# One Trainium2 core, decoder block: a merged opening, cross-attention scores by key, value products in three fp16 parts

## The reference

```python
x = x + attn(layernorm(x))                    # 128 heads, content 4 wide, rotary part 64 wide
x = x + xattn(layernorm(x), ctx, ctx, pos)    # 32 heads of 16, 8 key/value heads, rotary positions
x = x + ffn(layernorm(x))                     # 512x512 product, bias, top 2 of 8 low-rank experts
# cross-attention:
q = rope((x @ Wq)); k = rope((ctx @ Wk)); v = ctx @ Wv     # k, v repeated for 4 query heads each
probs = softmax(q @ k.T / 4)
x_out = (probs @ v) @ Wo
```

## Time and profile before

| | us |
|---|---|
| three runs | 902.01, 900.76, 896.24; median 900.76 |
| profiled execution, device time | 899.96 |
| its span, first to last instruction | 898.2 |
| busy in the span | PE 831.3, DVE 661.5, ACT 615.3, POOL 584.6 |
| mean granted TensorE clock | 0.974 of full |

### The profile page before, as it was taken

The page is one execution under the profiler, slowest core; times in us unless marked ns, Lnnn a source line. Parts: engine busy times, 40 slices in busy tenths (PEclk is TensorE's granted clock), DMA queues, the critical chain, the costliest instruction groups (busy, mean ns, idle before and its releaser), DMA issues. The chain is left out here.

```text
span 898.2 us, 18249 instructions
## 1 busy us (share of the span) xinstructions
PE 831.3 (93%) x5720; PEld 425.4 (47%) x5720; DVE 661.5 (74%) x1225; ACT 615.3 (68%) x1253; POOL 584.6 (65%) x491
## 2 busy tenths in 40 slices
PE   4968999999999999999999999999848889999996
PEld 3444444444444444444444444444313556666552
DVE  7877676767777888777888776887556667888764
ACT  4744777777777777777777777776602777777761
POOL 7824888878888887888788888876523341333210
PEclk9988999999999999999999999999979988999999
DMA  8341545543443334334333434422120000000000
GB/s 322 112 153 21 169 122 142 156 121 86 99 121 95 92 80 109 87 105 121 87 82 87 113 97 105 118 57 64 26 71 1 1 1 2 13 13 13 14 13 36
DMA packets 50719, 74.66 MB, mean 83 GB/s; under 512 B 9457, under 2 KB 33009, under 8 KB 50161
## 3 DMA queue, kind: packets, MB, share of 16 engines
q1 hardware_dynamic: 50672, 74.11, 29.7%
HBM read 38.16 MB, written 18.87 MB: 63 GB/s over the span
## 5 line engine op out<-in xcount | busy, mean ns | idle before, releaser
L480 POOL TENSOR_TENSOR Pl<-PR,Ph 128x512 f16<-128x512 f32 x254 | 286.2, 1158 | 30.0 <-ACT Ph L657 30.0
L650 ACT ACTIVATE PR<-PS 128x512 f32<-128x512 f32 x256 | 152.5, 597 | 129.7 <-PE PS L1266 123.2
L898 DVE TENSOR_REDUCE mneg<-PS 128x4 f32<-128x512 f32 x256 | 174.6, 685 | 38.2 <-PE PS L1246 34.7
L1197 PE MATMUL PS<-XTh,Wh 128*128 128x512 f16 x512 | 195.4, 382 | 0.0
L1197 PE MATMUL PS<-XTh,Wl 128*128 128x512 f16 x512 | 194.5, 380 | 0.0
L1197 PE MATMUL PS<-XTl,Wh 128*128 128x512 f16 x512 | 194.2, 379 | 0.0
L775 DVE SCALAR_TENSOR_TENSOR QS<-PS,QC 64x512 f16<-64x512 f32 x256 | 175.5, 686 | 18.9 <-ACT QC L578 11.9
L578 ACT ACTIVATE QC<-PS 64x512 f16<-64x512 f32 x256 | 150.7, 589 | 10.6 <-PE PS L1197 4.3
L657 ACT ACTIVATE Ph<-PR 128x512 f16<-128x512 f32 x256 | 139.3, 617 | 0.0
L1246 PEld LDWEIGHTS PS<-KC,QC 112*128 112x128 f16 x1024 | 79.0, 98 | 65.0 <-issue 5.9
L462 POOL TENSOR_TENSOR Wh<-Wraw,wscale 128x1024 f16<-128x1024 f32 x32 | 60.6, 1894 | 70.8 <-PE PS L1197 67.5
(11 more groups left out here) (211 smaller groups left out, 1281.8 us busy)
## 6 DMA issues: line engine op xcount, KB each, us to landing
Wraw<-in_wqr SPq DMA_DIRECT2D x32, 512.0 KB, 4.6
QS<-QC SPq DMA_DIRECT2D x64, 256.0 KB, 3.1
head_outputs<-OS SPq DMA_DIRECT2D x256, 40.0 KB
q_content_parts<-stg SPq DMA_DIRECT2D x12, 256.0 KB, 2.9
k_content_parts<-stg SPq DMA_DIRECT2D x12, 256.0 KB, 3.0
QC<-q_content_parts SPq DMA_DIRECT2D x128, 24.0 KB
KC<-k_content_parts SPq DMA_DIRECT2D x32, 96.0 KB
xs<-in_x SPq DMA_DIRECT2D x8, 256.0 KB, 4.7
```

The costliest lines, as they stand in the source:

```text
L480: nc.gpsimd.tensor_tensor(Pl[:, b], PR[:, b % 4], Ph[:, b], ALU.subtract).then_inc(s_pl, 1)
L650: nc.scalar.activation(PR[:, b % 4, :], PS[:, bB[b % 2], :], ACT.Exp, scale=ATT_SCALE).then_inc(s_e, 1)
L898: nc.vector.tensor_reduce(mneg[:, par, b // 4, :, b % 4], PS[:, bA[b % 2], :].rearrange("p (j k) -> p j k", j=GH), AX.X, ALU.max, negate=T ...
L1197: last = mm(PS[:, bQ[c % 2], :], wt[:, par, k, p * P:(p + 1) * P], xt[:, k, sl], start=(k == 0 and n == 0), stop=(k == KT - 1 and n == 2))
```

## The change

1. Opening: step 0 is gone. Each of the last four rounds of the loop over b on PE also issues one `rough_scores(0, 0, b - 4)`, with `row_max` behind the round's `up_low` on DVE; the first `max_turn` moves into step 1 behind its first projection, behind waits for the last `up_low` and `v_low`. The angles move to DVE's step 32, Sin to ACT behind the first weight split after the loop, the tables and both `k_rope` to DVE behind the weight splits. SP no longer waits for the key copies, and issues the first `q_again` by itself.
2. Second part: a unit's rough scores (8 products, both halves' row groups by turns), two maxima, one transpose of [128, 8] maxima, an ACT copy `xmT`, two small DMAs into row 48 of each half of `KQ`, scores by key (4 products of 256 columns, maximum subtracted by that row), Exp in 2 instructions of 512, high parts on ACT, low parts on POOL, and 12 fp16 value products. The 8 fp32 transposes of probabilities, their copies, the 8 Exp of 128 and the fp32 value product go. Rough scores run two units ahead. `x_back` comes behind `turn`. `KQ` has four buffers.
3. POOL writes high and low parts of `xvz`, and 16 into column 48 of `kst`. SP's result stores stand between the maxima's DMAs.

```diff
@@ -399,13 +401,12 @@
             contents(1, 1)
             store(1)
             store(2)
-            sp.wait_ge(s_kc, 2)
-            spelled(step, 0, 1)
+            q_again(0, 0, 0)
+            spelled(step, 1, 1)
             store(3)
             spelled(step, 2, 2)
...
-            for b in range(B):
+            def x_maxima(u):
+                sp.wait_ge(s_xme, u + 1)
+                for h in range(2):
+                    row = XROW * h + X3
+                    sp.dma_start(KQ[row:row + 1, u % 4, 0:UQ, :], xmT[REP * h:REP * (h + 1), u % 2, :]).then_inc(s_xmd[u % 2], 16)
+
...
+            for u in range(NU):
+                x_maxima(u)
+                if u % KT == KT - 1 and u // KT >= 3:
+                    result(u // KT - 3)
+            for b in range(B - 3, B):
+                result(b)
...
-            nc.gpsimd.memset(kst[:], 0.0)
+            nc.gpsimd.memset(kst[:], 0.0).then_inc(s_kx, 1)
             nc.gpsimd.memset(xvz[:], 0.0).then_inc(s_xvz, 1)
             nc.gpsimd.memset(qst[:], 0.0).then_inc(s_kx, 1)
+            pool.wait_ge(s_kx, 2)
+            nc.gpsimd.memset(kst[:, :, :, :, X3], MS).then_inc(s_kx, 1)
             pool.wait_ge(s_xvz, 1)
-            nc.gpsimd.tensor_copy(xvz[:, :, :, 0:XVC], xv[:]).then_inc(s_xvz, 1)
-            pool.wait_ge(s_kx, 1)
+            nc.gpsimd.tensor_copy(xvz[:, 0, :, :, 0:XVC], xv[:]).then_inc(s_xvz, 1)
+            pool.wait_ge(s_xvz, 2)
+            nc.gpsimd.tensor_tensor(xvz[:, 1, :, :, 0:XVC], xv[:], xvz[:, 0, :, :, 0:XVC], ALU.subtract).then_inc(s_xvz, 1)
+            pool.wait_ge(s_kx, 3)
...
@@ -564,6 +583,10 @@
                     nc.gpsimd.tensor_tensor(part[1], k, part[0], ALU.subtract).then_inc(s_kst, 1)
                 if r == 3:
                     inverse(2, b - 1)
+                if 0 <= u < NU:
+                    for h in range(2):
+                        pool.wait_ge(s_xph, 2 * u + h + 1)
+                        nc.gpsimd.tensor_tensor(XPl[:, u % 2, h], XPT[:, u % 2, h], XPh[:, u % 2, h], ALU.subtract).then_inc(s_xpl, 1)
...
@@ -681,6 +700,10 @@
             act.wait_ge(s_b, 8 * NG)
             for h, w in ((Wxh, wx_raw), (woh, xwo_sb), (bwh, bw_raw), (agh, ag_raw)):
                 nc.scalar.activation(h[:], w[:], ACT.Copy, scale=WS).then_inc(s_xh, 1)
+                if h is Wxh:
+                    act.wait_ge(s_red, 1)
+                    nc.scalar.activation(sincos[:].rearrange("p a b f -> p (a b f)"), red[:].rearrange("p a b f -> p (a b f)"),
+                                         ACT.Sin).then_inc(s_sc, 1)
...
+            def x_max_out(u):
+                if 0 <= u < NU:
+                    act.wait_ge(s_xmt, u + 1)
+                    if u >= 2:
+                        act.wait_ge(s_xmd[u % 2], 32 * (u // 2))
+                    nc.scalar.activation(xmT[:, u % 2, :], PS[0:2 * REP, 0, 3 * S:], ACT.Copy, scale=1 / MS).then_inc(s_xme, 1)
+
+            def x_exps(u, h):
+                if 0 <= u < NU:
+                    act.wait_ge(s_st, 2 * u + h + 1)
+                    if u >= 2:
+                        act.wait_ge(s_xpl, 2 * (u - 2) + h + 1)
+                    nc.scalar.activation(XPT[:, u % 2, h], PS[:, 4 + h, :], ACT.Exp).then_inc(s_ex, 1)
+
+            def x_high_parts(u):
+                if 0 <= u < NU:
+                    if u >= 2:
+                        act.wait_ge(s_xo, u - 1)
+                    for h in range(2):
+                        act.wait_ge(s_ex, 2 * u + h + 1)
+                        nc.scalar.activation(XPh[:, u % 2, h], XPT[:, u % 2, h], ACT.Copy).then_inc(s_xph, 1)
 
...
-                if 0 <= u < NU and r % 2 == 1:
-                    probs_out(u, 0)
+                x_max_out(u + 1)
+                x_exps(u, 0)
                 if 0 <= u - 1 < NU:
                     act.wait_ge(s_xo, u)
                     if u >= 2:
                         act.wait_ge(s_bk, u - 1)
                     nc.scalar.activation(OW[:], PS[:, 1, 0:2 * S], ACT.Copy).then_inc(s_ow, 1)
-                if 0 <= u + 1 < NU:
-                    exp_half(2 * u + 2)
-                if 0 <= u < NU:
-                    probs_out(u, 1)
-                if 0 <= u + 1 < NU:
-                    exp_half(2 * u + 3)
+                x_exps(u, 1)
+                x_high_parts(u)
 
         @block.vector
...
+                if b >= 4:
+                    up_low(8 + b)
+                    row_max(0, 0, b - 4)
+
...
@@ -923,6 +922,8 @@
                     o_out(g - 2, 0)
                 if g_is(g, NG + 1):
                     p_rest(g - 2)
+                if g_is(g, 1):
+                    max_out(0, 0)
                 for b in range(4, B):
                     if reached(g, 1, 1):
                         row_max(g - 1, 1 - par, b)
@@ -937,6 +938,8 @@
                     q_low(g, par, 1)
                 if reached(g, 2, 2):
                     o_out(g - 2, 1)
+                if g_is(g, NG):
+                    angles()
                 for b in range(4):
                     if reached(g, 0):
                         row_max(g, par, b)
@@ -947,8 +950,6 @@
                 apply_sums(g, 1)
                 if reached(g, 0):
                     max_out(g, 0)
-                if isinstance(g, int) and g == 0:
-                    k_rope(1)
 
             def share(g, t):
 
...
@@ -1069,8 +1092,6 @@
             dve.wait_ge(s_x1, 1)
             for u in range(FIRST, LAST):
                 b, r = (u + 1) // KT, (u + 1) % KT
-                if 0 <= u + 1 < NU:
-                    x_max(2 * u + 2)
                 if r == 1:
                     norm_low(2, b - 2, bF[0])
                     if 0 <= b - 3 < B:
@@ -1086,8 +1107,9 @@
                                             O2h[:, v % 2], ALU.subtract).then_inc(s_oTl, 1)
                 if r == 3:
                     norm_low(1, b + 2, bF[0])
-                if 0 <= u + 1 < NU:
-                    x_max(2 * u + 3)
+                if 0 <= u + 2 < NU:
+                    x_max(2 * u + 4)
+                    x_max(2 * u + 5)
                 if r == 3:
                     if 0 <= b - 1 < B:
                         v = b - 1
@@ -1095,8 +1117,6 @@
                         nc.vector.scalar_tensor_tensor(xs[:, v, :], PS[:, bF[1], :], 1 / WS, xs[:, v, :],
                                                        ALU.mult, ALU.add).then_inc(s_x2, 1)
                         dve.wait_ge(s_x2, v + 1)
-                if 0 <= u < NU and r % 2 == 0:
-                    p_turned(2 * u)
                 if 0 <= u - 1 < NU:
                     x_outputs(u - 1)
                 if r == 0:
...
 
             def scores(g, par, b):
                 t = b // 4
@@ -1288,6 +1307,10 @@
                     for n in range(8):
                         if reached(g, 1):
                             project(g, par, 2 * t + n // KT, n % KT)
+                        if g_is(g, 1) and t == 0 and n == 0:
+                            pe.wait_ge(s_ul, 16)
+                            pe.wait_ge(s_vl, B)
+                            max_turn(0, 0, 0)
                         if g_is(g, NG) and (t, n) in spare:
                             v, T = spare[t, n]
                             if v == 0 and T == 0:
...
+            def x_rough(u):
                 pe.wait_ge(s_kq, u + 1)
-                if n >= 2:
-                    pe.wait_ge(s_ex, n - 1)
-
-                r = XROW * (n % 2)
+                if u >= 1:
+                    pe.wait_ge(s_xm, 2 * u)
                 for j in range(REP):
-                    last = mm(PS[:, 2 + n % 2, j * S:(j + 1) * S], KQ[r:r + X3, u % 2, j], KQ[r:r + X3, u % 2, UQ + 2 * j // REP],
-                              start=True, stop=True)
-                last.then_inc(s_s, 1)
-
-            def turn_probs(n):
-                pe.wait_ge(s_ex, n + 1)
-                if n >= 2:
-                    pe.wait_ge(s_pe[n % 2], n // 2)
-                for j in range(REP):
-                    last = nc.tensor.transpose(PS[:, 4 + n % 2, j * S:(j + 1) * S], XP[:, n % 4, j], ident[:])
-                last.then_inc(s_pt, 1)
+                    for h in range(2):
+                        r = XROW * h
+                        last = mm(PS[:, 2 + h, j * S:(j + 1) * S], KQ[r:r + X3, u % 4, j], KQ[r:r + X3, u % 4, UQ + 2 * j // REP],
+                                  start=True, stop=True)
+                        if j == REP - 1:
+                            last.then_inc(s_s, 1)
+
+            def x_max_turn(u):
+                pe.wait_ge(s_xm, 2 * u + 2)
+                pe.wait_ge(s_kq, min(u + 2, NU))
+                nc.tensor.transpose(PS[0:2 * REP, 0, 3 * S:], xm[:, u % 2], ident[:]).then_inc(s_xmt, 1)
+
+            def x_scores(u):
+                pe.wait_ge(s_xmd[u % 2], 32 * (u // 2 + 1))
+                if u >= 1:
+                    pe.wait_ge(s_ex, 2 * u)
+                for g in range(2):
+                    for h in range(2):
+                        r = XROW * h
```

(60 more changed lines are left out.)

184 lines of the change are left out of this document (71 added, 113 removed).

## The result

The changed kernel takes 918.3 us (median of 4 runs, 916.9 to 922.1), against 900.6 us for the kernel before: the ratio is 1.021, with a 95% interval of 1.017 to 1.026. It is slower by more than 1%. The prediction was 912, slower, within 896 to 927. Executions of one and the same kernel differ: ten of the kernel before, measured beside e1 to e4, run from 895.1 us at a mean granted clock of 0.980 to 902.7 at 0.972, so a difference of 2 or 3 us between two profiled executions proves nothing by itself.

A forecast was written before the change was run, and what follows sets the result against it. PE was taken to bound main loop and second part, with POOL newly put into the second part's chain; 899.96 - 15 (opening) + 24.3 (second part with Exp's table load) + 2 (clock) = 911.3, forecast 912 us, range 896 to 927.

The forecast's parts named there:

- Opening, -15: Opening: PE's gap behind the angles goes and step 1 starts earlier at full clock, 15 us gained, bounds 12 to 17.
- Middle, 0: Between main loop and second part: tables and both k_rope fit DVE's 7.95 us wait for the gathered sums, costing 0.
- PE's work per unit: Second part: PE's work falls by 0.82 us a unit, 3.3 us a batch, to 19.3 us a batch.
- (a): Second part, r = 0: x_weigh waits for low parts queued on POOL behind the third-norm power, PE idles 2.9 us a batch.
- (b): Second part: the r = 1 unit's x_weigh waits for POOL's low parts, PE idles 1.8 us a batch.
- (c): Second part: only turn covers ACT's OW copy before x_back, four waits of 0.34 us, 1.35 us a batch.
- (d): Second part, r = 2: the transpose of the attention output waits 0.8 us for x_outputs, since x_back comes later.
- Clock, +2: Second part: half clock behind PE's waits costs 0 to 10 us in all, taken as 2.
- The rule on the shared port: DVE instructions with two SBUF inputs and POOL's SBUF reads exclude each other: 7 us worse, left in the range.
- Faster: Rival: PE stays the second part's bound and only its work counts, 863 us; chance 0.08.
- Balance: Rival: the second part loses as much as the opening gains, about 900 us; chance 0.30.
- The clock rival: Rival: half clock behind waits in the second part falls on the path, +10, 921 to 930 us; chance 0.20.

The follow-up runs named there:

- e1: The kernel before with only the changed opening and middle, its own second part kept: 882.9 us, ratio 0.982.
- e4: The changed kernel with the value product in fp32 again, no high and low parts of probabilities and values made: 871.1 us, ratio 0.968.
- e5: The changed kernel with 30 unread fp16 products on PE filling the r = 0 wait for low parts in seven batches: 920.0 us, ratio 1.023.
- e3: The changed kernel with POOL's third-norm power moved behind the unit's two low-part subtractions: 896.3 us, ratio 0.996.
- e6: e4 with ACT's high parts and POOL's low parts of the probabilities still made but read by no product: 884.9 us, ratio 0.983.
- e9: e5 with 13 more unread products filling PE's r = 2 wait for low parts too: 912.8 us, ratio 1.018.
- e7: The changed kernel without the probabilities' low parts: no POOL subtractions of them, 8 fp16 value products a unit, high parts kept: 872.1 us, ratio 0.970.
- e8: e4 with the value product ahead of the rough scores in PE's unit and ACT's OW copy first: 865.2 us, ratio 0.963.

## Why the prediction was right, and where it was off

- **Opening, -15: right.** -15.3 at the end of the main loop (14.4 to 16.5 over all runs with this opening), and e1 shows the gain by itself. Inside the sum two terms were off against each other: step 1 began 0.9 us later than the 60.4 worked out and its transpose 1.1 later than 62.4, which leaves 12.0 of the 13.1; so what followed gave 3.3 instead of 2.4. Before, the granted clock was 0.83 from 75 to 90 and it is 1.00 now, which is worth some 2.5 us; the other 0.8 has no place.
- **Middle, 0: off by 1.0, of which DVE is the smaller part.** The work was sized at 5.2 us in a cover of 7.95. It took 8.7 (639.30 to 648.00): 2.0 more for the pair beside POOL's subtraction, the rest in the tables (2.6 for 0.8). The step feared POOL's memsets for it, and they have a share: of the table operations, 0.18 us each where nothing stands beside them (e4), the first took 1.17 us and ended as POOL's memset did (640.47 and 640.42), the last 1.20 as POOL's cast did (641.85 and 641.80). The larger part was the new low part of `xvz`, which the step did not have. e4, which does not make that part, has the pair at 0.75 us and 2.43 us of the wait left, and its reciprocal starts 10.66 us after SP issues the first load of the sums, against 10.97 here (637.03 to 648.00) and 10.44 before (651.92 to 662.36). So DVE is late by about 0.3 (between 0.1 and 0.7, since the runs in which the wait is left have 10.24 to 10.88); the rest came in the transfers and the stores ahead of them, whose cause was not looked for. At the second part's start -14.4 is left.
- **Exp's table load, +1.3:** it is there, 1.28 us, at 681.35 on ACT. It stands ahead of the `KQ` copy for which PE waits 3.36 us at 685.52, so it lies in a wait of PE; no run is without it.
- **PE's work per unit: right in sign, too careful in size.** Starts in the trace after lie 0.33 us apart for the rough scores (0.50 predicted), 0.20 for the transpose (0.15), 0.32 for the scores (0.44), 0.45 for the twelve products (0.42): 1.30 instead of 1.51, which is 0.8 us a batch in the change's favour. It hardly showed, because PE was not the bound: in (a) PE's shorter work only lengthens its wait.
- **Waits: the mechanism right, the equal total partly luck.** (a) was given as 2.9 and (b) as 1.8 a batch, 33 us in all; they measured 3.85 and 0.70 in the batch shown, and 33.0 in all with some smaller waits of the first batches among them. (c), four waits of 0.34 for `OW`, is smaller: `x_back` starts 0.32 to 0.35 us behind the two `kst` transposes, which take 0.11, in three units of four, so 0.7 a batch for 1.35. (d) was given as 0.8 and is 0.74 (818.17). In (a) the chain from the end of `x_back` (799.35) to the low parts (806.65) took 7.3 for the 6.6 worked out, the 0.7 of it on DVE ahead of the statistics (they begin at 802.70, 3.35 in instead of 2.62), and PE, which goes on 0.15 later, had 3.6 us of work for the 3.7 worked out: 7.3 + 0.15 - 3.6 = 3.85. The slow products behind (a) shortened (b): without them, in e5, (b) is 1.65. e3 shows (a)'s cause, e4 and e6 that the dependence on the low parts is the larger part of the loss. For a batch without the slow clock the prediction gave 26.3 (its terms add up to 26.2); e9 has 26.56, with errors of PE's work (0.8) and of (c) (0.65) on one side and of the chain (0.7) on the other.
- **Clock, +2: the term most mis-sized.** By the profiled executions it is 6.2 (the changed kernel's second part less that of e9), by the medians 5.5 and by the ratios, whose intervals overlap, 2.5; so more than 2 is likely and the size is open, while the 1.03 us a batch is read from the trace. The step read "slow work beside a POOL wait costs nothing, otherwise up to 1.5 us a batch: 0 to 10, I take 2". But the slow `x_back` behind (a) stands ahead of DVE's `norm_rows(2)` and so of POOL's bias: POOL's walk to (b) starts late with it, and a batch takes 1.03 us more.
- **The sum.** For the profiled executions, opening and middle missed by 0.6, the second part with the waits filled by 2.6 (238.2 - 211.3 = 26.9 against 24.3), the clock by 4.2: together 7.4, from 911.3 to 918.65. The 2.6 are no more than the difference between e1's second part and before's, which are the same program.
- **The rule on the shared port, kept in the range at 7 us.** The POOL pair that meets `qr` took 2.81 us instead of 2.26 once a batch, so about 4 us along POOL's walk. By that rule (the Trainium skill, SBUF — State Buffer, "Who interferes with whom"), DVE should suffer as well as POOL; the runs agree: 153.6 against 135.0 us with and without the subtractions (e6, e7), and 2.75 against 0.75 for a pair with two SBUF inputs each. So do the groups: `eq` with two SBUF inputs goes from 218 to 819 ns, `pn` from 546 to 963, and the maxima, whose input is in PSUM, stay at 682 and 681. The prediction had this rule touch only `qr` and `norm_rows`, and only POOL's side of it; the comparisons of the gate on DVE were not foreseen. Its other example, the cast of 3.66 us, did end as POOL's memset beside it did (49.72 and 49.69), but a memset reads nothing, so that one goes beyond the rule as the prediction words it.
- **The rivals.** Faster fell: PE is not the bound with POOL in the chain. e4 and e8 are that rival with the low parts away, 871 and 865 us. Balance (900) is where e3 comes out. (The range's lower end, 896, was called balance's middle, though balance was put at about 900.) The clock rival was half right: it falls on the path, but with 2.5 to 6.2 us and not 10. That the opening would not shorten fell to e1.

What stays open: how e6's 13 us divide. PE's waits there grew for DVE and for ACT (`Al` 1.4 to 6.0, `rt` 2.6 to 5.0, `KQ` 4.8 to 8.2 against e4). The wait for `KQ` is 7.8 in e7 too, where no subtraction runs, so it comes with ACT's high parts; those for `Al` and `rt`, 1.4 and 2.6 in e7, come with the subtractions. How much of the time each is worth no run shows, since e7 also has a cheaper product. Of the 47 us, about 22 are the power's place (e3) and 13 the presence of the work (e6); some 12 are left, an estimate by difference, and e3 still waits 15.3 us for low parts.

## What to carry to other kernels

Before a precision split is put on another engine, read that engine's queue: here the largest part of the price, 22 of 47 us, was not the subtraction of 1.2 us but the order of one line, a one-column power ahead of it that waited 6.6 us for a third engine. Look also at what the work does to its neighbour: the subtractions lengthened DVE's by 18.6 us. Weigh what the split saves at its actual size: here 0.12 us of PE a unit. And where filling one wait of a cycle gains nothing, look whether the slow clock has gone or only moved before it is ruled out.

## What the runs showed of the hardware that was not expected

- With 256 columns and 32-wide outputs, the fp32 product is within 0.12 us of three fp16 ones: 0.57 (e4, 785.96 to 786.53) against 0.45 us (820.38 to 820.83) for the four groups of a unit.
- The half clock stood behind a wait of 3.85 us (e.g. 0.62 us for the operation at 806.80), and not behind one of 0.70 (0.40 at 820.38). In e5 it stood behind one of 1.65 (0.62 at 792.29), while behind another of 1.64 the operation at 764.67 took 0.40 and the slow one was the transpose 0.5 us later (0.61 at 765.20).
- 64 subtractions of 128x512 on POOL (e6 against e7) lengthened DVE's unchanged work by 18.6 us, some 0.3 us each. A single pair of DVE operations of 0.75 us took 2.75: it started 0.6 us behind one POOL subtraction of 128x1088, which took 2.75 too, and ended 0.6 us behind it. DVE's row maxima, which read PSUM, kept their 682 ns (681).
